# Decoder layer on one core: the operand buffers of TensorE moved to other addresses modulo 512 bytes

## The chip, the cores and the metric

The kernel runs on one core of a Trainium2 chip. The metric is the time on the device in microseconds (us); lower is better. Before the change the median of three runs was 2765.93 us (2765.84 to 2766.37).

## The reference

One decoder layer on x of 4 x 256 tokens and 512 features, with a context of 4 x 1601 tokens:

```
s = silu(x @ Wg.T); per token the 688 smallest |s| of 1376 are set to zero
x1 = layernorm(x + (s * (x @ Wu.T)) @ Wd.T)
q = rmsnorm(x1 @ Wq.T) per head (32 heads of 128);  k = rmsnorm(ctx @ Wk.T) (8 heads);  v = ctx @ Wv.T
x2 = layernorm(x1 + softmax(q @ k.T / sqrt(128) + mask) @ v @ Wo.T)   (1601 keys, 4 query heads a key head)
out = layernorm(x2 + the one chosen of 8 low-rank experts, rank 16)
```

## The kernel before, in words

All five engines run programs written out by hand, one after the other for six stages: gate and up projection, keys and values of the context (51 tiles of 128 tokens), down projection and norm, queries, attention (32 items of a batch and a key head, each in two units of two heads, 64 units in all), output projection with the experts. Semaphores set the order between engines; buffers have fixed places in the on-chip memory (SBUF).

Nearly every product is computed in three matmuls on operands split into a high and a low part of type float32r: hi by hi (line 158), hi by lo (159), lo by hi (160), in the helper `product` (lines 155 to 160). A matmul has a stationary operand of 128 x 128, which a weight load (PEld) brings into the array, and a moving operand of up to 512 columns, which streams through it. Each matmul has a weight load of its own. In a profile's row `banks<-kvw_hi,c_hi` the first name after the arrow is the moving operand and the second the stationary one.

Where the buffers stand: `chip.at(name, shape, place)` puts a tensor at byte 16512 + 4 x place of every partition, so place counts 4-byte words, and 128 words are 512 bytes. The constants AT_R0, AT_R1, AT_C, AT_X, AT_S and AT_P (16768, 28032, 39296, 43904, 46976, 49728) are multiples of 128 words, and so are the bare numbers in attention and output. Rows of 512, 1408 and 128 words keep it so. Before the change the moving and the stationary operand of every split matmul therefore start at the same place modulo 512 bytes: distance 0.

The buffers that the change touches, by stage:

- keys and values (`keys_and_values`): moving w_hi and w_lo (names kvw_hi, kvw_lo; one pair for K at AT_R0, one for V at AT_R1); stationary c_hi and c_lo, three slots used in turn, tile t in slot t mod 3; c_raw, which the DMA fills. Each tile makes 24 matmuls of 512 columns for K (2 blocks x 4 chunks x 3) and 24 for V.
- down projection: only p_sb (pd_sb), which makes room for V's buffer.
- attention (`attention`): moving k_hi and k_lo, two slots by item; stationary q_hi and q_lo. A score is 12 matmuls of 402 columns (4 blocks x 3), four scores a unit. The weighing of values (moving pT, stationary v) and the transposes (moving ident, stationary p_even or p_odd) are not touched.
- output (`output_and_experts`): moving wo_hi and wo_lo, eight pairs of buffers (QUAD_AT), one for each group of four heads; stationary o_hi and o_lo. 64 steps of 12 matmuls of 512 columns, eight steps with each pair.

The one product in which operands stood apart before is that of the experts at line 1926: expert_in's rows of 136 words start 0, 32, 64 and 96 bytes apart modulo 512 from x2T_sb.

Of the kernel before, what the change touches and what calls it, by code (L numbers as in the profile page):

```python
# [19 lines left out]
F32R = mybir.dt.float32r  # L20
U32 = mybir.dt.uint32

P = 128
B, S, D = 4, 256, 512
# [4 lines left out]
T = B * S  # L29
TT = T // P  # L30
CT = D // P
# [18 lines left out]
AT_ABS = 5760  # L50
AT_R0 = 16768
AT_R1 = 28032
AT_C = 39296
# [279 lines left out]
def keys_and_values(chip, abs_s, k_sb, WkT, WvT, ctxT, kS, vS, down):  # L333
# [7 lines left out]
    NB = N // 512  # L341
    RING = 3
# [4 lines left out]
    raw = chip.raw.rearrange("p (r n) -> p r n", r=IC)  # L347
    w_raw, first_c = raw[:, 0:SLOTS], raw[:, SLOTS].rearrange("p (c n) -> p c n", c=CT)
    sources = (WkT, WvT)
    w_hi = [chip.at(f"kvw_hi{m}", [P, NB, CT, 512], place, F32R) for m, place in enumerate((AT_R0, AT_R1))]  # L350
    w_lo = [chip.at(f"kvw_lo{m}", [P, NB, CT, 512], place + NB * CT * 512, F32R)
            for m, place in enumerate((AT_R0, AT_R1))]
    TAIL = 2 * NB * CT * 512
    flags = chip.at("flags", [P, 2, I], AT_R0 + TAIL, BF16)
    order = chip.at("order", [P, I], AT_R0 + TAIL + I)
    c_raw = chip.at("c_raw", [P, RING, CT, P], AT_C)

    HI_AT, LO_AT = (5, 6, 3), (7, 8, 4)
    c_hi = [chip.at(f"c_hi{s}", [P, CT, P], AT_C + 512 * HI_AT[s], F32R) for s in range(RING)]
    c_lo = [chip.at(f"c_lo{s}", [P, CT, P], AT_C + 512 * LO_AT[s], F32R) for s in range(RING)]  # L360
    square = chip.at("square", [P, N], AT_X)
    v_sb = chip.at("v_sb", [P, 2, N], AT_S)
    kT_sb = chip.at("kT_sb", [P, 2, N], AT_P)
# [329 lines left out]
def down_and_norm(chip, keep, x1T_hi, x1T_lo, x, WdT, pS, x1S, k_sb, queries):  # L693
# [3 lines left out]
    w_hi = chip.at("wd_hi", [P, IC, D], AT_R0, F32R)  # L697
    w_lo = chip.at("wd_lo", [P, IC, D], AT_R0 + IC * D, F32R)
    GN = IC * P
    hT_hi = [chip.at(f"hT_hi{s}", [P, GN], AT_C + GN * s, F32R) for s in range(2)]  # L700
    hT_lo = [chip.at(f"hT_lo{s}", [P, GN], AT_C + GN * (2 + s), F32R) for s in range(2)]
    p_sb = chip.at("pd_sb", [P, 2, GN], AT_R1 + 2 * CT * T)
    x_sb = chip.at("xd_sb", [P, 2, D], AT_X + 2 * 1024)
    y_sb = chip.at("yd_sb", [P, 2, D], AT_SMALL - 2 * D)
    x1_sb = chip.at("x1_sb", [P, 2, D], AT_X + 1024)
# [290 lines left out]


def queries(chip, x1T_hi, x1T_lo, WqT, qn, kn, qS, attention):


# [219 lines left out]
def attention(chip, mask, qS, kS, vS, oS, output):  # L1220
# [10 lines left out]
    SB, SW = 4, 402  # L1231
# [6 lines left out]
    RING = 4  # L1238
# [13 lines left out]
    p_sb = [chip.at("p_even", [P, QT, PP], 9088), chip.at("p_odd", [P, QT, PP], AT_R1)]  # L1252

    def pair(name, shape, *places):
        return [chip.at(f"{name}{s}", [P, *shape], place, F32R) for s, place in enumerate(places)]

    k_hi = pair("k_hi", (SB, 512), AT_C, AT_R0)
    k_lo = pair("k_lo", (SB, 512), AT_C + SB * 512, AT_R0 + SB * 512)
    q_hi = pair("q_hi", (2 * QW,), AT_C + 2 * SB * 512, AT_R0 + 2 * SB * 512)
    q_lo = pair("q_lo", (2 * QW,), AT_C + 2 * SB * 512 + 2 * QW, 48768)  # L1260
    v_hi = pair("v_hi", (NT * HD,), 45440, 49792)
# [403 lines left out]
def output_and_experts(chip, oS, x1S, WoT, AT, routeT, BwT, out):  # L1665
# [8 lines left out]
    W = 4 * P  # L1674
    RING = 3
    LEAD = RING - 1
    w_raw = raw[:, 0:WR * 2 * D].rearrange("p (r h n) -> p r h n", r=WR, h=2)
    o_raw = raw[:, WR * 2 * D:WR * 2 * D + OR * W].rearrange("p (r n) -> p r n", r=OR)
    QUAD_AT = (AT_C, AT_C + 8 * D, AT_ABS, AT_ABS + 8 * D, AT_ABS + 16 * D, 25088, 25088 + 8 * D, 25088 + 16 * D)
    w_hi = [chip.at(f"wo_hi{c}", [P, 4, D], QUAD_AT[c], F32R) for c in range(QUADS)]  # L1680
    w_lo = [chip.at(f"wo_lo{c}", [P, 4, D], QUAD_AT[c] + 4 * D, F32R) for c in range(QUADS)]
    o_hi = chip.at("o_hi", [P, RING, W], 22016, F32R)
    o_lo = chip.at("o_lo", [P, RING, W], 22016 + RING * W, F32R)
    y1_sb = chip.at("y1_sb", [P, 2, D], 18048)
    y2_sb = chip.at("y2_sb", [P, 2, D], 18048 + 2 * D)
    x2_sb = chip.at("x2_sb", [P, 2, D], 18048 + 4 * D)
# [258 lines left out]
def decoder_layer(nc, x, xT, ctxT, mask, WgT, WuT, WdT, WqT, WkT, WvT, WoT, qn, kn, routeT, AT, BwT, out):  # L1945
# [7 lines left out]
    with ExitStack() as whole:  # L1953
# [4 lines left out]
        x1T_lo = chip.at("x1T_lo", [P, CT, T], AT_R1 + CT * T, F32R)  # L1958

        output = output_and_experts(chip, oS, x1S, WoT, AT, routeT, BwT, out)  # L1960
        attend = attention(chip, mask, qS.rearrange("b g d h q -> (b g) d (h q)"), kS, vS, oS, output)
        query = queries(chip, x1T_hi, x1T_lo, WqT, qn, kn, qS, attend)
        down = down_and_norm(chip, abs_s, x1T_hi, x1T_lo, x, WdT, pS, x1S, k_sb, query)
        keys = keys_and_values(chip, abs_s, k_sb, WkT, WvT, ctxT, kS, vS, down)
        gate = gate_and_up(chip, abs_s, xT, WgT, WuT, pS, keys)

# [95 lines left out]
```

## Time and profile before

| | |
|---|---|
| median of three runs | 2765.93 us |
| time of the profiled execution | 2767.25 us |
| its span, first to last instruction | 2765.5 us |
| TensorE (PE) busy | 2722.0 us, 98% |
| weight loads (PEld) busy | 2364.3 us, 85% |
| VectorE, ScalarE, GpSimd busy | 74%, 49%, 37% |
| share of PE in the chain that ended last | 96% |
| granted TensorE clock, mean | 0.995 |

A matmul's record in the profile lasts from its start until its result is out, so the records of consecutive matmuls overlap; what a matmul costs is the time from its start to the start of the next. The timeline gives starts to 0.01 us, so a mean over several is read from the first and the last start of a stretch.

### The profile page before, as it was taken

The numbers are of one execution on the slowest core, as the hardware profiler recorded it, in microseconds if no ns is written. First come the engines' busy times: TensorE is split into PE (matmuls) and PEld (weight loads), VectorE is DVE, ScalarE is ACT, GpSimd is POOL, SyncE is SP. The second block draws the span as 40 slices with busy tenths as digits, with TensorE's granted clock in tenths as the row PEclk, the third lists the DMA queues.
The fourth block names the chain that finished last, engine by engine and source line by source line (L and its number), as shares of the span: only waits on it lengthen the run. The fifth ranks groups of instructions, "written<-read, shape, count | busy, mean of one in ns | idle before, by whom it ended". The sixth has DMA issues, their size and how long they took to land.

```text
span 2765.5 us, 45347 instructions
## 1 busy us (share of the span) xinstructions
PE 2722.0 (98%) x14624; PEld 2364.3 (85%) x14624; DVE 2055.5 (74%) x3054; ACT 1361.5 (49%) x2992; POOL 1009.9 (37%) x752
## 2 busy tenths in 40 slices
PE   8999999999999999999999999999999999999998
PEld 7888888888788878998998998999999999898786
DVE  2299999988855557777777777777777777777543
ACT  3243343334424445565666566666656666655421
POOL 1122222223313345444545444454444454541000
PEclk9999999999999999999999999999999999999999
DMA  5253333333333443111111111111111111111632
GB/s 177 83 181 108 112 111 107 114 114 114 95 124 114 125 128 98 55 53 54 51 60 55 62 55 62 55 62 55 62 55 58 52 49 58 55 43 61 210 107 73
DMA packets 252783, 239.49 MB, mean 87 GB/s; under 512 B 12084, under 2 KB 210772, under 8 KB 252728
## 3 DMA queue, kind: packets, MB, share of 16 engines
q1 hardware_dynamic: 252728, 238.81, 27.9%
q8 instruction: 28, 0.46, 0.1%
q14 instruction: 27, 0.22, 0.0%
HBM read 142.92 MB, written 95.85 MB: 86 GB/s over the span
## 4 chain that ended last, share of the span: by engine, by line
PE 96%; issue 2%; DVE 1%; POOL 1%; ACT 0%; DMA 0%; POOLq 0%; SPq 0%; DVEq 0%; ACTq 0%
PE banks L158 27%; PE banks L160 26%; PE banks L159 26%; PE banks L1616 13%; PE banks L322 2%; PE banks L1194 1%; PE banks L929 0%; PE banks L1926 0%; PE banks L1936 0%; POOL rstd_q L1094 0%; DVE p_even L1534 0%; DMA raw<-WoT_in 0%; POOL p_even L1427 0%; POOL x_lo L230 0%; DVE wo_lo L1825 0%
## 5 line engine op out<-in xcount | busy, mean ns | idle before, releaser
L1573 DVE TENSOR_TENSOR pT_lo<-banks,pT_hi 128x512 fp32r<-128x512 f32 (+1 forms) x832 | 573.6, 690 | 110.6 <-ACT pT_hi L1503 94.9
L1503 ACT CAST pT_hi<-banks 128x512 fp32r<-128x512 f32 (+1 forms) x576 | 333.7, 580 | 529.4 <-PE banks L1616 529.2
L559 DVE TENSOR_SCALAR_CACHE_REDUCE flags<-abs_s,cand 128x1376 bf16<-128x1376 f32 x248 | 393.2, 1642 | 1.1
L158 PE MATMUL banks<-k_hi,q_hi 128*128 128x402 f32 x1024 | 379.9, 371 | 0.0
L158 PE MATMUL banks<-pT_hi,v_hi 128*128 128x512 f32 (+1 forms) x832 | 374.0, 450 | 2.9 <-DVE pT_lo L1573 1.7
L159 PE MATMUL banks<-k_lo,q_hi 128*128 128x402 f32 x1024 | 357.2, 349 | 0.0
L160 PE MATMUL banks<-k_hi,q_lo 128*128 128x402 f32 x1024 | 355.8, 347 | 0.0
L160 PE MATMUL banks<-pT_hi,v_lo 128*128 128x512 f32 (+1 forms) x832 | 327.5, 394 | 0.0
L159 PE MATMUL banks<-pT_lo,v_hi 128*128 128x512 f32 (+1 forms) x832 | 326.6, 393 | 0.0
L1427 POOL TENSOR_SCALAR p_even<-p_even,p_inv 128x1601 f32<-128x1601 f32 x128 | 207.1, 1618 | 320.0 <-DVE p_inv L1541 320.0
L158 PE MATMUL banks<-kvw_hi,c_hi 128*128 128x512 f32 x816 | 322.6, 395 | 0.0
L160 PE MATMUL banks<-kvw_hi,c_lo 128*128 128x512 f32 x816 | 318.7, 391 | 0.0
L159 PE MATMUL banks<-kvw_lo,c_hi 128*128 128x512 f32 x816 | 317.9, 390 | 0.0
L1534 DVE CUSTOM_DVE_ANT_0 p_odd<-banks,minus_mask 128x1608 f32<-128x1608 f32 x128 | 234.6, 1833 | 105.4 <-PE banks L160 105.4
L1534 DVE CUSTOM_DVE_ANT_0 p_even<-banks,minus_mask 128x1608 f32<-128x1608 f32 x128 | 234.6, 1833 | 104.4 <-PE banks L160 104.4
L1427 POOL TENSOR_SCALAR p_odd<-p_odd,p_inv 128x1601 f32<-128x1601 f32 x128 | 206.9, 1617 | 211.4 <-DVE p_inv L1541 211.3
L1616 PEld LDWEIGHTS banks<-ident,p_even 128*128 128x128 f32 (+1 forms) x1664 | 207.9, 140 | 56.6 <-DVE qT_sb L1160 2.0
L1616 PEld LDWEIGHTS banks<-ident,p_odd 128*128 128x128 f32 (+1 forms) x1664 | 206.9, 140 | 55.9 <-POOL p_odd L1427 1.0
L1616 PE MATMUL banks<-ident,p_even 128*128 128x128 f32 (+1 forms) x1664 | 250.3, 273 | 1.8 <-DVE qT_sb L1160 1.8
L1616 PE MATMUL banks<-ident,p_odd 128*128 128x128 f32 (+1 forms) x1664 | 249.3, 272 | 0.6 <-POOL p_odd L1427 0.6
L1481 ACT ACTIVATE p_odd<-p_odd,t_min 128x1601 f32<-128x1601 f32 x128 | 209.9, 1640 | 41.3 <-DVE t_min L1534 41.3
L1481 ACT ACTIVATE p_even<-p_even,t_min 128x1601 f32<-128x1601 f32 x128 | 209.6, 1638 | 30.6 <-DVE t_min L1534 30.6
(160 smaller groups left out, 5316.2 us busy)
## 6 DMA issues: line engine op xcount, KB each, us to landing
raw<-keys SPq DMA_DIRECT2D x32, 800.5 KB, 4.5
values<-v_sb SPq DMA_DIRECT2D x50, 512.0 KB, 2.6
keys<-kT_sb SPq DMA_DIRECT2D x50, 512.0 KB, 4.4
raw<-values SPq DMA_DIRECT2D x32, 768.0 KB
queries<-qT_sb SPq DMA_DIRECT2D x64, 256.0 KB, 2.6
raw<-queries SPq DMA_DIRECT2D x32, 512.0 KB, 5.2
attended<-o_sb SPq DMA_DIRECT2D x128, 128.0 KB, 1.9
raw<-attended SPq DMA_DIRECT2D x64, 256.0 KB, 2.8
```

What stands on the lines that cost most here:

```text
L158: pe.matmul(out, a_hi, b_hi, start=start, stop=False)
L159: pe.matmul(out, a_hi, b_lo, start=False, stop=False)
L160: return pe.matmul(out, a_lo, b_hi, start=False, stop=stop)
L322: last = pe.transpose(banks[:, g * P:(g + 1) * P], k_sb[:, g * HD:(g + 1) * HD], chip.ident)
L559: bits.done(dve.tensor_scalar(flags[:, tt % 2], abs_s[:, tt], at[:, tt:tt + 1].bitcast(F32), 0.0, ALU.is_lt, ALU.add, accum_out=out[:, tt: ...
L1194: last = pe.transpose(psum[:, bank(i, s), h * P:(h + 1) * P], q_sb[:, s % 4, h * HD:(h + 1) * HD], ident)
L1427: pool.tensor_scalar(at, at, p_inv[:, n:n + 1], 1.0, ALU.mult, ALU.mult).then_inc(p_done, 1)
L1481: act.activation(at, at, ACT.Exp, bias=t_min[:, n:n + 1], scale=-1.0, accum_out=p_sum[:, n:n + 1]).then_inc(e_done, 1)
L1503: act.copy(pT_hi[0:rows(kt), m % RING], t_bank(m)[0:rows(kt)]).then_inc(pT_hi_act, 1)
L1534: dve.tensor_tensor_reduce(banked(p_sb[u % 2][:, j, 0:KP]), psum[:, 0:SB, 0:SW], banked(minus_mask[:, j % 2]), 1.0, 3.4028235e38, ALU.add, ...
L1573: dve.tensor_tensor(pT_lo[0:rows(kt), m % RING], t_bank(m)[0:rows(kt)], pT_hi[0:rows(kt), m % RING].bitcast(F32), ALU.subtract).then_inc(p ...
L1616: last = pe.transpose(t_bank(m)[0:rows(kt), P * j:P * (j + 1)], p_sb[u % 2][:, j, P * kt:P * kt + rows(kt)], ident)
```

## The change

Nothing is added, removed or put in another order: each engine's instruction rows are the same in both kernels, but for line numbers. Only places change. In words (of 4 bytes, modulo 128): V's moving weights go 64 up; the stationary slots of the context 8 down, 0 and 24 down, and c_raw 32 down; pd_sb one whole period of 128 up; k_hi and k_lo of the odd slot 40 down; the eight pairs of wo_hi and wo_lo 88, 24, 64, 48, 8, 80, 56 and 40 down; o_hi and o_lo one whole period down.

```
@@ -347,17 +347,18 @@
     raw = chip.raw.rearrange("p (r n) -> p r n", r=IC)
     w_raw, first_c = raw[:, 0:SLOTS], raw[:, SLOTS].rearrange("p (c n) -> p c n", c=CT)
     sources = (WkT, WvT)
-    w_hi = [chip.at(f"kvw_hi{m}", [P, NB, CT, 512], place, F32R) for m, place in enumerate((AT_R0, AT_R1))]
+    W_AT = (AT_R0, AT_R1 + 64)
+    w_hi = [chip.at(f"kvw_hi{m}", [P, NB, CT, 512], place, F32R) for m, place in enumerate(W_AT)]
     w_lo = [chip.at(f"kvw_lo{m}", [P, NB, CT, 512], place + NB * CT * 512, F32R)
-            for m, place in enumerate((AT_R0, AT_R1))]
+            for m, place in enumerate(W_AT)]
     TAIL = 2 * NB * CT * 512
     flags = chip.at("flags", [P, 2, I], AT_R0 + TAIL, BF16)
     order = chip.at("order", [P, I], AT_R0 + TAIL + I)
-    c_raw = chip.at("c_raw", [P, RING, CT, P], AT_C)
-
-    HI_AT, LO_AT = (5, 6, 3), (7, 8, 4)
-    c_hi = [chip.at(f"c_hi{s}", [P, CT, P], AT_C + 512 * HI_AT[s], F32R) for s in range(RING)]
-    c_lo = [chip.at(f"c_lo{s}", [P, CT, P], AT_C + 512 * LO_AT[s], F32R) for s in range(RING)]
+    c_raw = chip.at("c_raw", [P, RING, CT, P], AT_C - 32)
+
+    SLOT_AT = (AT_C + 5 * 512 - 8, AT_C + 7 * 512, AT_C + 3 * 512 - 24)
+    c_hi = [chip.at(f"c_hi{s}", [P, CT, P], SLOT_AT[s], F32R) for s in range(RING)]
+    c_lo = [chip.at(f"c_lo{s}", [P, CT, P], SLOT_AT[s] + 512, F32R) for s in range(RING)]
     square = chip.at("square", [P, N], AT_X)
     v_sb = chip.at("v_sb", [P, 2, N], AT_S)
     kT_sb = chip.at("kT_sb", [P, 2, N], AT_P)
@@ -699,7 +700,7 @@
     GN = IC * P
     hT_hi = [chip.at(f"hT_hi{s}", [P, GN], AT_C + GN * s, F32R) for s in range(2)]
     hT_lo = [chip.at(f"hT_lo{s}", [P, GN], AT_C + GN * (2 + s), F32R) for s in range(2)]
-    p_sb = chip.at("pd_sb", [P, 2, GN], AT_R1 + 2 * CT * T)
+    p_sb = chip.at("pd_sb", [P, 2, GN], AT_R1 + 2 * CT * T + P)
     x_sb = chip.at("xd_sb", [P, 2, D], AT_X + 2 * 1024)
     y_sb = chip.at("yd_sb", [P, 2, D], AT_SMALL - 2 * D)
     x1_sb = chip.at("x1_sb", [P, 2, D], AT_X + 1024)
@@ -1254,8 +1255,8 @@
     def pair(name, shape, *places):
         return [chip.at(f"{name}{s}", [P, *shape], place, F32R) for s, place in enumerate(places)]
 
-    k_hi = pair("k_hi", (SB, 512), AT_C, AT_R0)
-    k_lo = pair("k_lo", (SB, 512), AT_C + SB * 512, AT_R0 + SB * 512)
+    k_hi = pair("k_hi", (SB, 512), AT_C, AT_R0 - 40)
+    k_lo = pair("k_lo", (SB, 512), AT_C + SB * 512, AT_R0 - 40 + SB * 512)
     q_hi = pair("q_hi", (2 * QW,), AT_C + 2 * SB * 512, AT_R0 + 2 * SB * 512)
     q_lo = pair("q_lo", (2 * QW,), AT_C + 2 * SB * 512 + 2 * QW, 48768)
     v_hi = pair("v_hi", (NT * HD,), 45440, 49792)
@@ -1676,11 +1677,12 @@
     LEAD = RING - 1
     w_raw = raw[:, 0:WR * 2 * D].rearrange("p (r h n) -> p r h n", r=WR, h=2)
     o_raw = raw[:, WR * 2 * D:WR * 2 * D + OR * W].rearrange("p (r n) -> p r n", r=OR)
-    QUAD_AT = (AT_C, AT_C + 8 * D, AT_ABS, AT_ABS + 8 * D, AT_ABS + 16 * D, 25088, 25088 + 8 * D, 25088 + 16 * D)
+    QUAD_AT = (AT_C - 88, AT_C + 8 * D - 24, AT_ABS - 64, AT_ABS + 8 * D - 48, AT_ABS + 16 * D - 8,
+               24832 + 256 - 80, 25088 + 8 * D - 56, 25088 + 16 * D - 40)
     w_hi = [chip.at(f"wo_hi{c}", [P, 4, D], QUAD_AT[c], F32R) for c in range(QUADS)]
     w_lo = [chip.at(f"wo_lo{c}", [P, 4, D], QUAD_AT[c] + 4 * D, F32R) for c in range(QUADS)]
-    o_hi = chip.at("o_hi", [P, RING, W], 22016, F32R)
-    o_lo = chip.at("o_lo", [P, RING, W], 22016 + RING * W, F32R)
+    o_hi = chip.at("o_hi", [P, RING, W], 21888, F32R)
+    o_lo = chip.at("o_lo", [P, RING, W], 21888 + RING * W, F32R)
     y1_sb = chip.at("y1_sb", [P, 2, D], 18048)
     y2_sb = chip.at("y2_sb", [P, 2, D], 18048 + 2 * D)
     x2_sb = chip.at("x2_sb", [P, 2, D], 18048 + 4 * D)
```

## Rows read from the trace of the kernel before

**Rows 1.** Page: busy time, share and instructions; granted clock; shares of the chain.

```profile
PE 2722.0 (98%) x14624; PEld 2364.3 (85%) x14624; DVE 2055.5 (74%) x3054; ACT 1361.5 (49%) x2992; POOL 1009.9 (37%) x752
...
PEclk9999999999999999999999999999999999999999
...
PE 96%; issue 2%; DVE 1%; POOL 1%; ACT 0%; DMA 0%; POOLq 0%; SPq 0%; DVEq 0%; ACTq 0%
```

**Rows 2.** Groups by line and shape: matmuls touched, with busy and mean ns.

```profile
L158 PE MATMUL banks<-k_hi,q_hi 128*128 128x402 f32 x1024 | 379.9, 371 | 0.0
...
L158 PE MATMUL banks<-kvw_hi,c_hi 128*128 128x512 f32 x816 | 322.6, 395 | 0.0
...
L158 PE MATMUL banks<-wo_hi,o_hi 128*128 128x512 f32 x256 | 105.1, 410 | 2.1 <-DVE wo_lo L1825 2.1
```

**Rows 3.** Timeline of PE in keys and values: start us, us, what.

```profile
399.85 0.39 PE L158 MATMUL banks<-kvw_hi,c_hi 128*128 128x512 f32 x1
400.07 0.39 PE L159 MATMUL banks<-kvw_lo,c_hi 128*128 128x512 f32 x1
...
403.93 0.39 PE L158 MATMUL banks<-kvw_hi,c_hi 128*128 128x512 f32 x1
```

**Rows 4.** The same groups' weight loads, and those of the transposes.

```profile
L159 PEld LDWEIGHTS banks<-k_lo,q_hi 128*128 128x128 f32 x1024 | 196.0, 191 | 0.0
...
L1616 PEld LDWEIGHTS banks<-ident,p_odd 128*128 128x128 f32 x1536 | 191.1, 140 | 51.5 <-POOL p_odd L1427 1.0
...
L159 PEld LDWEIGHTS banks<-kvw_lo,c_hi 128*128 128x128 f32 x816 | 153.5, 188 | 30.3
```

**Rows 5.** Timeline of PE over one score of attention.

```profile
1502.24 0.35 PE L159 MATMUL banks<-k_lo,q_hi 128*128 128x402 f32 x1
...
1502.99 0.34 PE L160 MATMUL banks<-k_hi,q_lo 128*128 128x402 f32 x1
1503.16 0.34 PE L158 MATMUL banks<-k_hi,q_hi 128*128 128x402 f32 x1
1503.34 0.35 PE L159 MATMUL banks<-k_lo,q_hi 128*128 128x402 f32 x1
...
1504.28 0.39 PE L158 MATMUL banks<-pT_hi,v_hi 128*128 128x512 f32 x1
```

**Rows 6.** Timeline of PE in gate and up.

```profile
104.45 0.40 PE L158 MATMUL banks<-w_hi,x_hi 128*128 128x512 f32 x1
...
105.16 0.39 PE L158 MATMUL banks<-w_hi,x_hi 128*128 128x512 f32 x1
105.38 0.39 PE L159 MATMUL banks<-w_lo,x_hi 128*128 128x512 f32 x1
...
105.85 0.32 PE L158 MATMUL banks<-w_hi,x_hi 128*128 128x352 f32 x1
```

**Rows 7.** Timeline of PE around transposes of keys.

```profile
645.85 1.04 PE L322 MATMUL banks<-ident,k_sb 128*128 128x128 f32 x8
646.65 0.47 PE L158 MATMUL banks<-kvw_hi,c_hi 128*128 128x512 f32 x1
```

**Rows 8.** Timeline of PE in the output stage, around the experts' product.

```profile
2657.77 0.39 PE L159 MATMUL banks<-wo_lo,o_hi 128*128 128x512 f32 x1
...
2660.30 1.09 PE L1926 MATMUL banks<-expert_in,x2T_sb 128*128 128x136 f32 x8
2661.14 0.48 PE L158 MATMUL banks<-wo_hi,o_hi 128*128 128x512 f32 x1
```

**Rows 9.** Three stretches: busy us by engine: keys, attention, output.

```profile
core 0: us, PE busy (x) PEld busy (x) DVE busy (x) ACT busy (x) POOL busy (x), PEclk, DMA share, GB/s
160.00:700.00 540.00, 540.00 (x2567) 450.85 (x2566) 501.45 (x687) 211.90 (x874) 149.77 (x138) 1.00 0.38 113
1044.00:2526.00 1482.00, 1481.54 (x8701) 1337.31 (x8702) 1167.92 (x1817) 896.31 (x1282) 709.96 (x405) 1.00 0.19 58
2600.00:2720.00 120.00, 120.00 (x555) 97.46 (x554) 57.33 (x128) 28.09 (x51) 6.98 (x12) 1.00 0.35 106
```

More of the change, by code:

```diff
@@ L349, in keys_and_values @@
     sources = (WkT, WvT)
-    w_hi = [chip.at(f"kvw_hi{m}", [P, NB, CT, 512], place, F32R) for m, place in enumerate((AT_R0, AT_R1))]
+    W_AT = (AT_R0, AT_R1 + 64)
+    w_hi = [chip.at(f"kvw_hi{m}", [P, NB, CT, 512], place, F32R) for m, place in enumerate(W_AT)]
     w_lo = [chip.at(f"kvw_lo{m}", [P, NB, CT, 512], place + NB * CT * 512, F32R)
-            for m, place in enumerate((AT_R0, AT_R1))]
+            for m, place in enumerate(W_AT)]
     TAIL = 2 * NB * CT * 512
@@ L355, in keys_and_values @@
     order = chip.at("order", [P, I], AT_R0 + TAIL + I)
[L356 to L360, printed above, removed]
+    c_raw = chip.at("c_raw", [P, RING, CT, P], AT_C - 32)
+    SLOT_AT = (AT_C + 5 * 512 - 8, AT_C + 7 * 512, AT_C + 3 * 512 - 24)
+    c_hi = [chip.at(f"c_hi{s}", [P, CT, P], SLOT_AT[s], F32R) for s in range(RING)]
+    c_lo = [chip.at(f"c_lo{s}", [P, CT, P], SLOT_AT[s] + 512, F32R) for s in range(RING)]
     square = chip.at("square", [P, N], AT_X)
@@ L701, in down_and_norm @@
     hT_lo = [chip.at(f"hT_lo{s}", [P, GN], AT_C + GN * (2 + s), F32R) for s in range(2)]
-    p_sb = chip.at("pd_sb", [P, 2, GN], AT_R1 + 2 * CT * T)
+    p_sb = chip.at("pd_sb", [P, 2, GN], AT_R1 + 2 * CT * T + P)
     x_sb = chip.at("xd_sb", [P, 2, D], AT_X + 2 * 1024)
@@ L1255, in pair @@
         return [chip.at(f"{name}{s}", [P, *shape], place, F32R) for s, place in enumerate(places)]
-    k_hi = pair("k_hi", (SB, 512), AT_C, AT_R0)
-    k_lo = pair("k_lo", (SB, 512), AT_C + SB * 512, AT_R0 + SB * 512)
+    k_hi = pair("k_hi", (SB, 512), AT_C, AT_R0 - 40)
+    k_lo = pair("k_lo", (SB, 512), AT_C + SB * 512, AT_R0 - 40 + SB * 512)
     q_hi = pair("q_hi", (2 * QW,), AT_C + 2 * SB * 512, AT_R0 + 2 * SB * 512)
@@ L1678, in output_and_experts @@
     o_raw = raw[:, WR * 2 * D:WR * 2 * D + OR * W].rearrange("p (r n) -> p r n", r=OR)
-    QUAD_AT = (AT_C, AT_C + 8 * D, AT_ABS, AT_ABS + 8 * D, AT_ABS + 16 * D, 25088, 25088 + 8 * D, 25088 + 16 * D)
+    QUAD_AT = (AT_C - 88, AT_C + 8 * D - 24, AT_ABS - 64, AT_ABS + 8 * D - 48, AT_ABS + 16 * D - 8,
+               24832 + 256 - 80, 25088 + 8 * D - 56, 25088 + 16 * D - 40)
     w_hi = [chip.at(f"wo_hi{c}", [P, 4, D], QUAD_AT[c], F32R) for c in range(QUADS)]
     w_lo = [chip.at(f"wo_lo{c}", [P, 4, D], QUAD_AT[c] + 4 * D, F32R) for c in range(QUADS)]
-    o_hi = chip.at("o_hi", [P, RING, W], 22016, F32R)
-    o_lo = chip.at("o_lo", [P, RING, W], 22016 + RING * W, F32R)
+    o_hi = chip.at("o_hi", [P, RING, W], 21888, F32R)
+    o_lo = chip.at("o_lo", [P, RING, W], 21888 + RING * W, F32R)
     y1_sb = chip.at("y1_sb", [P, 2, D], 18048)
```

## The prediction

> **What bounds the kernel now.** I read the page first: TensorE is busy for 98% of the span and makes up 96% of the chain that ended last, at a granted clock of 9 tenths or more in every slice, which is the 2.4 GHz level [rows 1]. So the time is the number of matmuls times the time from one start to the next. Then the groups by line and shape, for the counts [rows 2]. Their mean of 371 to 410 ns is no cost, since the records overlap; the cost has to be read from the starts in the timeline. In the keys stage 18 matmuls of 512 columns follow each other from 399.85 to 403.93, 4.08 us, that is 226.7 ns each, with line 158, 159 and 160 alike [rows 3]. At 2.4 GHz 512 columns stream in 512 / 2.4 = 213.3 ns, so 13.3 ns of each are something else. In a score 11 matmuls of 402 columns go from 1502.24 to 1504.28, 2.04 us, 185.5 ns each [rows 5], against 402 / 2.4 = 167.5: 18.0 ns are something else. The excess does not grow with the columns, so it goes with the matmul, and each matmul has a weight load of 128 columns beside it.
>
> Next I asked whether the excess is contention between the two streams that read on-chip memory. Two rows speak for it. A weight load takes 188 to 191 ns beside a split matmul and 140 beside a transpose, 48 to 51 ns less [rows 4]. And matmuls of one shape, all at distance 0, do not all cost the same: in a score two in a row take 0.35 us (175 ns each, from 1502.99 to 1503.34), the last five 0.94 (188 each) [rows 5]; in the gate stage one takes 0.22 us (105.16 to 105.38) while six around it take 1.40 (233.3 each) [rows 6]; in the output stage, after an interruption, 11 take 2.53 (230.0 each, 2657.77 to 2660.30) [rows 8]. Something that depends on how the two streams fall against each other in time moves a 512-column matmul between about 220 and 233 ns and a 402-column one between 175 and 188. A distance in the address could act on the same thing. That it does is not shown by any row.
>
> **The change, part by part.** No instruction is added, removed or reordered on any engine, and sizes and counts stay, so only durations can change.
>
> Matmuls whose distance changes: K's projection in slots 0 and 2, 34 of 51 tiles x 24 = 816; slot 1 keeps distance 0 (17 x 24 = 408 do not change). V's projection, all 51 x 24 = 1224. Scores of the odd slot: 16 of 32 items x 2 units x 4 scores x 12 = 1536, half of the 3072, three lines of 1024 each [rows 2]. The output projection, 64 x 12 = 768, three lines of 256 each [rows 2]. That is 2808 matmuls of 512 columns and 1536 of 402, 4344 of 14624 [rows 1]. The moves of o_hi, o_lo and pd_sb are by a whole period and cost nothing at any distance; the gate, down and query stages, the weighing of values and the transposes keep distance 0.
>
> The price of one is not in the trace, since no split matmul stands at another distance there. I bound it from both sides.
> - Fastest: if the excess went entirely, 2808 x 13.3 = 37.3 us and 1536 x 18.0 = 27.6 us, 65 us in all. The best that the trace shows for such shapes is 0.22 us and 175 ns [rows 5, 6]; with 0.22 taken at its full 6.7 ns below 226.7 that is 2808 x 6.7 = 18.8 us and 1536 x 10.5 = 16.1 us, 35 us in all.
> - Slowest: the slow stretches, 233.3 and 188.0 ns [rows 5, 6]: 2808 x 6.6 = 18.5 us and 1536 x 2.5 = 3.8 us, 22 us in all. Nothing excludes that a bad distance costs more than any stretch at distance 0. As an outer end, the weight load's own 48 ns [rows 4] on every one of them would be 4344 x 48 = 209 us; I give it little weight, since the excess at distance 0 is a quarter of that.
>
> The value I take: eight different distances will not all be the best one, so a third of the 35 us of the best stretches, 12 us. The reason for the sign is that at distance 0 both streams begin at the same place modulo 512 at the same time: the weight load that follows starts with the matmul before it, in nearly every case, and its 512 bytes and the first 512 bytes of the moving row coincide. A distance takes that coincidence away. It is a weak reason, and I say so.
>
> Other engines don't take this gain away. In the keys stretch VectorE is busy 501.45 of 540 us, in attention 1167.92 of 1482, in the output stage 57.33 of 120, while TensorE fills all three [rows 9]. The closest cover is in the keys stage: VectorE could follow a TensorE that is up to 7% faster (38.55 / 540), and even the whole excess is 13.3 / 226.7 = 5.9%. So a gain on TensorE there is a gain of the kernel. A loss is one in any case.
>
> The sum against the profiled execution: 2767.25 - 12 = 2755; that execution is 1.3 us above the median of the runs (2765.93), so in terms of the median 2754.
>
> One rule speaks against the change. The row: of 226.7 ns per matmul, 13.3 are not streaming [rows 3]. The Trainium skill, TensorE: Matmul & The Clock Gate, section "Step-by-step: what each phase is for", says that the engine has two independent read ports and that loading the next weights takes no read bandwidth from the running matmul; by that no address can matter. By that rule the time stays at 2766. The same page, "LDWEIGHTS (loading the stationary operand)", sets 128 columns at 128 / 1.2 = 107 ns; the trace has 140 and 188 ns, longer beside a full-rate stream, which the rule does not account for, so it does not settle the matter.
>
> **The rivals.**
> - No change. The excess is a price of swapping weights, or of two streams that share something whatever their addresses. For it: the streams move at different rates (the moving one reads 2048 bytes in the time of a matmul, the weight load 512), so each passes the other modulo 512 whatever distance they start at, and a distance would only say when. Also the only product at other distances, that of the experts with 0, 32, 64 and 96 bytes, takes 0.84 us for eight of 136 columns, and the transposes of keys at distance 0 take 0.80 for eight of 128 [rows 7, 8]: 1.05 against 136 / 128 = 1.06, so no distance is felt there. But those run at half the rate (about 100 ns for 128 columns against 53 at 2.4 GHz), where there may be nothing to collide. Against it: the spread between 175 and 188 ns at one and the same distance. The time: 2766.
> - Slower. At distance 0 the matmul leaves the weight load behind from the first column; at a distance at which the load's place lies a little ahead, the moving stream runs into it and stays behind it. The place is the start of each of the 4344 matmuls. It decides once the mean over the new distances is more than 1.3 ns above now (5.5 us / 4344). For it: the long runs in keys sit at 226.7, below the 230 and 233 of unsettled stretches [rows 3, 6, 8], so distance 0 is already a good state there, and a spread of distances is more likely to be worse than a good state than better. Against it: scores do not sit at a good state, and they go down to 175. Price: half of the slow stretches to all of them, 11 to 22 us; I take 14: 2780. A bad distance beyond what rows show would give 2790 and more.
> - The full gain: every new distance takes the excess away. For it only the 175 ns in a score, which is 7.5 above streaming. 2766 - 65 to 2766 - 35 is 2701 to 2731.
>
> **How the numbers follow.** Two executions differ by some tenths of a us, and 0.2%, 5.5 us, is about what a measurement tells from no change. Faster by a part (2735 to 2760) 0.33, and by the full gain 0.08: faster 0.41. No change 0.26. Slower 0.33, of which 0.08 is beyond 2788. The likeliest single one is the part gain, 2754. The range leaves out the full gain and the far slow end, and little more: 2730 to 2788. The likeliest case's own range is 2735 to 2760.
>
> **What would show it.** Start to start in the timeline, by stage. If I am right, V's projection and the output stage lie below 226.7 ns, with differences between the eight groups of the output stage; scores of odd items lie below 185.5 on average and those of even items stay; K's slot 1 stays at 226.7 while slots 0 and 2 move. The weight loads' 188 to 191 ns fall where the starts come closer. If all stay, the first rival holds. If untouched matmuls (gate, transposes, values) move, my whole account of where the effect can act is wrong; if VectorE gets waits in the keys stage, its cover was thinner than the busy share says.

## The result: slower by 0.85%

The changed kernel takes 2789.97 us in the median of four runs (2789.73 to 2791.42), the kernel before 2766.15 beside it; the ratio is 1.0085, with a 95% interval of 1.0073 to 1.0097. The forecast was 2754 us, within 2730 to 2788. The time lies just above the range, and on the other side of no change: a gain was forecast and a loss came.

The page of the changed kernel first: busy time by engine, granted clock, shares of the chain.

```profile
PE 2744.1 (98%) x14624; PEld 2365.4 (85%) x14624; DVE 2055.2 (74%) x3054; ACT 1362.8 (49%) x2992; POOL 1011.6 (36%) x752
...
PEclk9999999999999999999999999999999999999999
...
PE 95%; issue 2%; DVE 1%; POOL 1%; ACT 0%; DMA 0%; SPq 0%; POOLq 0%; DVEq 0%; ACTq 0%
```

Against [rows 1] nothing moved but TensorE: its span is 2787.9 us (2765.5 before), its busy time 22.1 us longer with the same 14624 matmuls, the clock at the same level, VectorE and the others within 2 us. The same three stretches as in [rows 9], busy us by engine:

```profile
core 0: us, PE busy (x) PEld busy (x) DVE busy (x) ACT busy (x) POOL busy (x), PEclk, DMA share, GB/s
160.00:700.00 540.00, 540.00 (x2524) 443.03 (x2523) 492.88 (x682) 208.23 (x855) 147.12 (x136) 1.00 0.37 111
1044.00:2526.00 1482.00, 1474.98 (x8600) 1325.09 (x8601) 1156.15 (x1799) 889.83 (x1274) 714.97 (x410) 1.00 0.19 58
2600.00:2720.00 120.00, 120.00 (x542) 96.20 (x542) 59.32 (x121) 32.61 (x54) 5.92 (x10) 1.00 0.39 126
```

TensorE still fills the stretches of keys and output and begins 2524 matmuls instead of 2567 in the first and 542 instead of 555 in the last. (The second stretch now begins before attention runs at full pace, since everything is later.) So the time went into the matmuls themselves, and the timeline of TensorE shows into which. K's projection of one tile in slot 0 and of the next in slot 1, first and last row of each, then V's in slot 1, its third, twelfth and last row:

```profile
492.41 0.40 PE L158 MATMUL banks<-kvw_hi,c_hi 128*128 128x512 f32 x1
...
497.77 0.39 PE L160 MATMUL banks<-kvw_hi,c_lo 128*128 128x512 f32 x1
...
504.48 0.39 PE L158 MATMUL banks<-kvw_hi,c_hi 128*128 128x512 f32 x1
...
509.69 0.40 PE L160 MATMUL banks<-kvw_hi,c_lo 128*128 128x512 f32 x1
...
511.26 0.40 PE L160 MATMUL banks<-kvw_hi,c_lo 128*128 128x512 f32 x1
...
513.34 0.39 PE L160 MATMUL banks<-kvw_hi,c_lo 128*128 128x512 f32 x1
...
516.06 0.40 PE L160 MATMUL banks<-kvw_hi,c_lo 128*128 128x512 f32 x1
```

K in slot 0, 8 words off, takes 5.36 us (497.77 - 492.41) for 23 matmuls, 233 ns each; K in slot 1, which kept distance 0, takes 5.21, 226.5 ns, as in [rows 3]. V in slot 1 stands 64 words (256 bytes) off and takes 4.80 us for 21, 228.6 ns: 231.1 in the first nine of them, soon after an interruption by transposes, and 226.7 in the last twelve (2.72 us). At a distance of 8 words no such flat stretch comes: by the unrounded starts of this trace K in slot 0 repeats 235, 233, 234, 231 ns to the end of its run. So the distance decides into which pattern a run falls.

Two scores of the odd slot, one right after the other, ten starts each:

```profile
1749.47 0.34 PE L159 MATMUL banks<-k_lo,q_hi 128*128 128x402 f32 x1
...
1751.32 0.35 PE L160 MATMUL banks<-k_hi,q_lo 128*128 128x402 f32 x1
...
1754.04 0.35 PE L159 MATMUL banks<-k_lo,q_hi 128*128 128x402 f32 x1
...
1756.05 0.37 PE L160 MATMUL banks<-k_hi,q_lo 128*128 128x402 f32 x1
```

That is 1.85 and 2.01 us, 184 (1.842 us by the unrounded starts) and 201 ns per matmul, at one and the same distance; in [rows 5] it was 185. And in the output stage two of the eight groups, 40 words off (first pair) and 16 modulo 64 (second pair):

```profile
2648.08 0.39 PE L159 MATMUL banks<-wo_lo,o_hi 128*128 128x512 f32 x1
...
2650.41 0.40 PE L160 MATMUL banks<-wo_hi,o_lo 128*128 128x512 f32 x1
...
2657.80 0.39 PE L159 MATMUL banks<-wo_lo,o_hi 128*128 128x512 f32 x1
...
2660.09 0.40 PE L160 MATMUL banks<-wo_hi,o_lo 128*128 128x512 f32 x1
```

233 and 229 ns. Every start of the trace taken together (means from the start of a matmul to the next start, in ns, from unrounded starts; interrupted ones left out):

| group | distance in words (moving - stationary) | before | after | matmuls |
|---|---|---|---|---|
| K slot 0, 2 | 8, 24 | 226.8, 226.7 | 233.4, 233.4 | 816 |
| K slot 1 | 0 | 226.7 | 226.7 | 408 |
| V slot 0, 2 | 72, 88 | 227.8, 227.9 | 233.4, 233.1 | 816 |
| V slot 1 | 64 | 227.8 | 228.5 | 408 |
| scores, odd items | 88 | 185.0 | 190.1 | 1536 |
| scores, even items | 0 | 184.9 | 184.9 | 1536 |
| output, groups 0 to 7 | 40, 104, 64, 80, 120, 48, 72, 88 | 227.0 to 229.7 | 233.2, 234.3, 230.4, 228.9, 233.1, 233.4, 232.9, 234.3 | 96 each |

816 x 6.7 = 5.5 us for K, 816 x 5.4 + 408 x 0.7 = 4.7 for V, 1536 x 5.1 = 7.8 for scores, and 768 at a mean of 4.5 in the output make 3.5: 21.5 of the 22.4 us by which the span grew. Not all of that is as neat as it looks. With the interrupted starts counted too, keys and values take 10.0 us more, scores 6.4 (594.6 to 601.0), the output stage 1.8, and the weighing of values, which the change does not touch, 2.8 (625.2 to 628.0; 228.7 to 231.4 ns each). But attention at its old places comes in two states: in the kernels below that leave it alone, scores take 592.4 and 591.8 us and the weighing of values 627.6 and 627.9 (keys only, output only), the same sum as 594.6 and 625.2 to 0.2 us. Against those kernels attention lost 9 us, nearly all of it in scores.

The weight loads, whose times I had taken for a sign of contention [rows 4], still take 191, 140 and 188 ns:

```profile
L159 PEld LDWEIGHTS banks<-k_lo,q_hi 128*128 128x128 f32 x1024 | 196.0, 191 | 1.0
...
L1617 PEld LDWEIGHTS banks<-ident,p_odd 128*128 128x128 f32 x1536 | 191.2, 140 | 51.9 <-POOL p_odd L1428 1.0
...
L159 PEld LDWEIGHTS banks<-kvw_lo,c_hi 128*128 128x128 f32 x816 | 153.3, 188 | 33.6
```

### The profile page after: what moved, and what is told of

The parts are those of the page before. It is cut to its first block, busy times and chain, and to the rows that moved or that the text cites. A ratio compares the mean times of both kernels' runs of the same rounds, so it can differ in the third digit from the quotient of the medians.

```text
span 2787.9 us, 45347 instructions
## 1 busy us (share of the span) xinstructions
PE 2744.1 (98%) x14624; PEld 2365.4 (85%) x14624; DVE 2055.2 (74%) x3054; ACT 1362.8 (49%) x2992; POOL 1011.6 (36%) x752
## 4 chain that ended last, share of the span: by engine, by line
PE 95%; issue 2%; DVE 1%; POOL 1%; ACT 0%; DMA 0%; SPq 0%; POOLq 0%; DVEq 0%; ACTq 0%
PE banks L158 27%; PE banks L160 26%; PE banks L159 26%; PE banks L1617 13%; PE banks L322 2%; PE banks L1195 1%; PE banks L930 0%; DMA raw<-WoT_in 0%; PE banks L1928 0%; PE banks L1938 0%; POOL rstd_q L1095 0%; DVE p_even L1535 0%; POOL p_even L1428 0%; DVE wo_lo L1827 0%; DVE p_odd L1535 0%
```

## The experiments

Each ran beside the kernel before on the same chip. The parts and the pair are measured in several runs each; the kernels with half loads, other load lengths or narrower rows leave out a part of the products, so they were run once, and only their starts are read. First the question whether it is the distance at all.

**Both operands moved alike.** K's and V's weights and the context slots, k and q of the odd slot, and all operands of the output stage stand 88 words (40 down, which is the same modulo 128) off their old places, so the distance is 0 again. Three buffers of other engines and q_lo of the odd slot move to make room. Lines of the edit against the kernel before, others left out (...):

```
-    ... for m, place in enumerate((AT_R0, AT_R1))]
+    ... for m, place in enumerate((AT_R0 + 88, AT_R1 + 88))]
...
+    SLOT_AT = (AT_C + 5 * 512 - 40, AT_C + 7 * 512 - 40, AT_C + 3 * 512 - 40)
...
-    k_hi = pair("k_hi", (SB, 512), AT_C, AT_R0)
+    k_hi = pair("k_hi", (SB, 512), AT_C + (0), AT_R0 + (88))
...
+    q_hi = pair("q_hi", (2 * QW,), AT_C + 2 * SB * 512, AT_R0 + 2 * SB * 512 + 88)
+    q_lo = pair("q_lo", (2 * QW,), AT_C + 2 * SB * 512 + 2 * QW, 24064 + 88)
...
+    QUAD_AT = (AT_C - 40, AT_C + 8 * D - 40, AT_ABS - 40, ...
+    o_hi = chip.at("o_hi", [P, RING, W], 21976, F32R)
```

> Here the places of both operands move by the same 88 (or 40 down) words in keys and values, in the odd items of attention and in the output stage, so no start stands on a multiple of 256 bytes, and the distance is 0 everywhere. Theory D (only the distance between moving and stationary operand counts): start to start stays 226.7 ns in the settled runs of keys and values and in the output stage, 185 ns in scores of both slots, and the kernel takes 2766 us, as before. Theory P (an operand that starts off a multiple of 256 bytes is read more slowly, by itself): 233 ns and 190 ns as in the changed kernel, also where that kernel kept 226.7 (K of slot 1, 408 matmuls), and at least 2790 us.

Measured: 2767.42 us, ratio 0.9998 (0.9988 to 1.0007). K of slot 0 in the timeline, first and last of its 24 matmuls:

```profile
487.20 0.39 PE L158 MATMUL banks<-kvw_hi,c_hi 128*128 128x512 f32 x1
...
492.41 0.39 PE L160 MATMUL banks<-kvw_hi,c_lo 128*128 128x512 f32 x1
```

5.21 us for 23 matmuls, 226.5 ns; over all tiles K has 226.7 in every slot, and scores of the odd slot 184.2. V has 228.4 to 228.5 for 227.8 before, a difference that lies in the ten matmuls after each interruption. So at this place, 88 words on, the place by itself costs next to nothing; the distance does. Theory P falls.

**Other distances.** The same edits with other numbers; four of the output groups use a distance that is no multiple of 8 words, by a slice of a buffer that is allocated a little lower. The places in short (a list, not the code):

```
w_hi, w_lo: AT_R0, AT_R1 + 32;  SLOT_AT: -16, 0, -32;  k_hi, k_lo: AT_C - 16, AT_R0 - 32
QUAD_AT: -112, -96, -124, -116, -68, -108, -32, -16
```

> Other distances (moving minus stationary, words): K 16, 0, 32 and V 48, 32, 64 in slots 0, 1, 2; scores -16 in even items, -32 in odd ones; output groups 16, 32, 4, 12, 60, 20, 96, 112. Theory D with a period of 256 bytes (64 words), as the changed kernel's groups suggest: V slot 2 (64) stays at 226.7, like K slot 1 (0); V slot 0 (48) is at 233; K slot 0, output groups 0 and 7 at 16 and 112 (48) give 229 and 233; the not yet measured 32 and 96 are alike, and by that theory K slot 2, V slot 1 and output groups 1 and 6 agree within 1 ns. With a period of 512 bytes 32 and 96 differ, and so do 0 and 64. Rival T (the distance acts only on timing, each group's mean is one of many states): the groups of one distance differ among stages. Whole kernel: between 2770 and 2790 us by D; no value below 226.7 is expected by the thought that 0 is the best state, one or more below it if 0 is only one state among many.

Measured: 2780.58 us, ratio 1.0042 (1.0026 to 1.0059). K in slot 0 (16 words), K in slot 2 (32), V in slot 2 (64):

```profile
491.89 0.39 PE L158 MATMUL banks<-kvw_hi,c_hi 128*128 128x512 f32 x1
...
497.16 0.39 PE L160 MATMUL banks<-kvw_hi,c_lo 128*128 128x512 f32 x1
...
515.77 0.39 PE L158 MATMUL banks<-kvw_hi,c_hi 128*128 128x512 f32 x1
...
521.14 0.39 PE L160 MATMUL banks<-kvw_hi,c_lo 128*128 128x512 f32 x1
...
522.71 0.39 PE L160 MATMUL banks<-kvw_hi,c_lo 128*128 128x512 f32 x1
...
527.51 0.39 PE L160 MATMUL banks<-kvw_hi,c_lo 128*128 128x512 f32 x1
```

5.27 us for 23 (229 ns), 5.37 (233 ns) and 4.80 for 21 (229 ns). With the groups of the changed kernel, the means by distance modulo 64 words (one word is 4 bytes) are as follows, with 0 standing for the places of the kernel before and 64 for moved groups:

| distance, words | 0 | 64 | 4 | 8 | 12 | 16 | 20 | 24 | 32 | 40 | 48 | 56 | 60 |
|---|---|---|---|---|---|---|---|---|---|---|---|---|---|
| ns at 512 columns | 226.7 (K), 227.8 (V), 227.0 to 229.7 (output) | 228.5, 228.9 (V), 230.4 (output) | 231.7 | 232.9 to 233.4 | 232.5 | 228.9 to 229.1 | 231.1 | 233.1 to 234.3 | 231.9 to 233.1 | 233.2, 234.3 | 232.6 to 233.4 | 233.1 | 235.9 |

Where groups of different stages share a distance other than 0 modulo 64 they agree within 1.2 ns, and groups at 64 words lie only 0.7 to 1.1 ns above their own value at 0 (V slot 1 and output group 2 of the changed kernel, V slot 2 here, where theory D had expected 226.7; V moved alike at distance 0 also had 228.5), so the period is 256 bytes, not 512, and rival T falls for matmuls of 512 columns. The state is not wholly the group's own: K's slot 1, still at 0, has 227.6 in this kernel. By the unrounded starts its runs begin with 226, 235, 228, 234, 231 ns and stay near 226.7 from about the eighth matmul on; in the changed kernel, where they follow an unsettled run of V as well, they have 226.7 from the start. Of K's and V's runs in this trace too only those at 0 and 64 words reach that value; the others end in patterns of their own, K at 16 words in one of 225 to 233 ns, K at 32 in one of 228 to 239. Of the distances tried none is better than 0 at 512 columns; 16 words (64 bytes) come next. Scores take 186.0 ns at 32 words (odd items) and 183.4 at 48 (even items).

**The parts alone.** Each with the diff of the change for that stage and the other stages as before.

> The change in keys and values alone. Theory D: K slots 0 and 2 and V slots 0 and 2 at 233.2 to 233.4 ns, slot 1 at 226.7 and 228.5, the rest as before: 4 x 408 matmuls x 6.2 ns = 10 us, so 2776 us. If the stages influenced each other (VectorE later in keys, for one), it would be another sum.

Measured: 2776.66 us, ratio 1.0030 (1.0018 to 1.0042); profiled span 2775.0, 9.5 more than before. All six slots as in the changed kernel within 0.1 ns.

> The change of k_hi and k_lo of the odd slot alone. Theory D: scores of odd items at 190.1 ns for 185.0, 1536 x 5.1 = 7.8 us, and the matmul after a score up to 2 us in all: 2774 to 2776 us. Rival: the loss in attention is taken up by slack there (TensorE idles 0.5 of 1482 us there before, so hardly any): 2766 to 2768.

Measured: 2777.18 us, ratio 1.0035 (1.0023 to 1.0046); span 2775.4, 9.9 more. Odd scores 189.8 ns, even ones 184.9: TensorE has no slack that takes this loss up.

> The change of the output stage alone: the eight groups as in the changed kernel (233 ns but for those at 64 and 80 words, at 230.4 and 228.9), 96 matmuls each, 3 to 4 us in all: 2769 to 2770 us. With keys alone (+9.5) and attention alone (+10) the sum makes the whole change's 22 to 24 us if the parts do not influence each other.

Measured: 2770.91 us, ratio 1.0012 (1.0002 to 1.0021); span 2770.0, 4.5 more. The groups are within 0.5 ns of the changed kernel's. The three spans add up to 23.9 us, the whole change to 22.4. Single executions of one kernel differ by more than these 1.5 us (2763.8 to 2769.3 for the span of the kernel before, run beside the keys and attention kernels), so no influence of the parts on each other is seen.

**Is it what the weight load reads?** Half of the stationary columns from the second tile on, first at the old places, then at the changed ones. This leaves out half of the rows of each product (a memset of the banks at the start makes the rows that are not written defined):

```
-    last = product(pe, out[:, j * 512:(j + 1) * 512], c_hi[s % RING][:, c], c_lo[s % RING][:, c],
+    m = P if first else P // 2
+    last = product(pe, out[0:m, j * 512:(j + 1) * 512], c_hi[s % RING][:, c, 0:m], c_lo[s % RING][:, c, 0:m],
```

> From tile 1 on, keys and values load only 64 of the 128 stationary columns and so compute only half of each product's rows (the other rows keep older values); places are those of the kernel before, distance 0. Moving columns stay 512. Theory L (the excess over 213.3 ns is what the weight load's reads take from the moving stream): about half as many reads, so the settled start to start falls from 226.7 to about 220 ns. Rival W (a fixed price of swapping weights): it stays at 226.7.

Measured: 2771.80 us in one run. The weight loads of 64 columns, then K in slot 0 at distance 0:

```profile
L159 PEld LDWEIGHTS banks<-kvw_lo,c_hi 128*64 128x64 f32 x800 | 107.5, 134 | 71.3
```

```profile
490.79 0.40 PE L158 MATMUL banks<-kvw_hi,c_hi 128*64 128x512 f32 x1
...
496.08 0.40 PE L160 MATMUL banks<-kvw_hi,c_lo 128*64 128x512 f32 x1
```

The load takes 134 ns for 188, but the matmuls take 5.29 us for 23, 230 ns: more than with the whole load, not less. Theory L fails, and so does the rival W, which expected 226.7.

> The same halved weight loads, at the changed kernel's places. Theory L: the loss by distance halves as well: slots 0 and 2 at about 223 to 224 ns, 3 above slot 1 (6.7 with full loads). Rival W: slots 0 and 2 keep the full 6.7 ns above slot 1. A second rival: a distance only matters where the two streams start together, then the difference is independent of the load's length too.

Measured: 2786.53 us in one run. K in slot 0 (8 words) and in slot 1 (0):

```profile
491.74 0.39 PE L158 MATMUL banks<-kvw_hi,c_hi 128*64 128x512 f32 x1
...
497.05 0.39 PE L160 MATMUL banks<-kvw_hi,c_lo 128*64 128x512 f32 x1
...
503.69 0.39 PE L158 MATMUL banks<-kvw_hi,c_hi 128*64 128x512 f32 x1
...
508.98 0.39 PE L160 MATMUL banks<-kvw_hi,c_lo 128*64 128x512 f32 x1
```

5.31 and 5.29 us; over the tiles with half loads 230.8, 230.0 and 231.4 ns for slots 0, 1 and 2. The loss by distance nearly goes, but because distance 0 loses its advantage. Neither rival had said so.

**Widths.** The places of the changed kernel, with narrower moving rows in keys and values from the second tile on, so that the rest of the output's columns is left out; in the next run (384, 416) stands for (448, 402):

```
+    n = 512 if first else (448, 402)[which]
+    ... out[:, j * 512:j * 512 + n], ..., w_hi[which][:, j, c, 0:n], w_lo[which][:, j, c, 0:n]
```

> Places of the changed kernel; from tile 1 on K's matmuls stream 448 of 512 columns and V's 402 (the rest of the output keeps older values), with whole weight loads. Slots 0 and 2 stand 8 and 24 words off modulo 64, slot 1 stands at 0. Theory M (a matmul settles at streaming + 13.3 ns if its distance and its width are multiples of 64 words, and otherwise wanders about 16 to 20 ns over streaming): K slot 1 at 448 / 2.4 + 13.3 = 200.0 ns, K slots 0 and 2 at 203 to 207; V slot 1 at 402 / 2.4 + 16 to 18 = 184 to 185.5, as the scores of the kernel before, V slots 0 and 2 at 187 to 190. Rival N (width is of no account, the scores' higher excess comes from something else in attention): V slot 1 at 167.5 + 13.3 = 180.8.

Measured: 2747.48 us in one run. V with 402 columns in slot 1, 21 matmuls apart:

```profile
487.30 0.34 PE L160 MATMUL banks<-kvw_hi,c_lo 128*128 128x402 f32 x1
...
491.16 0.34 PE L160 MATMUL banks<-kvw_hi,c_lo 128*128 128x402 f32 x1
```

3.86 us, 183.8 ns. Over the narrowed tiles 183.7 in slot 1, 184.5 and 188.5 in slots 0 and 2; K with 448 columns has 204.7, 203.0 and 205.3 in slots 0, 1 and 2. So at 402 columns 8 words cost V only 0.8 ns, less than theory M had. By the unrounded starts a run of V in slot 1 goes 189, 184, 176, 179, 183, 186, 191, 187, 185, 175, 180, ... ns, the sequence of the scores of the kernel before (186, 190, 188, 185, 176, 178, 183, 186, 191, 188). So the scores' higher excess over streaming comes from their width, and rival N falls; but 448 at distance 0 is 203.0, not the settled 200.0 that theory M had.

> The same with K's matmuls 384 wide and V's 416. Theory M: K slot 1 at 160 + 13.3 = 173.3 ns and settled, V slot 1 (416 is no multiple of 64) at 173.3 + 16 to 18 = 189 to 191. Rival N: V slot 1 at 186.6.

Measured: 2751.47 us in one run. K with 384 columns in slot 0, 8 words off:

```profile
468.72 0.34 PE L158 MATMUL banks<-kvw_hi,c_hi 128*128 128x384 f32 x1
...
472.71 0.34 PE L160 MATMUL banks<-kvw_hi,c_lo 128*128 128x384 f32 x1
```

3.99 us for 23, 173.5 ns; over the narrowed tiles 173.3, which is 13.3 above the 160.0 of streaming (384 / 2.4) and settled, at a distance that is bad for 512 columns. (The settled values at 384 and 512 columns, 173.3 and 226.7, differ by 53.4 ns for 128 columns, which is 2.4 columns a ns; that is the sense in which 13.3 ns are not streaming.) Slot 1 (distance 0) has a mean of 174.6 and settles at 173.3 late in a run, slot 2 has 176.5; V with 416 has 187.4, 188.3 and 193.0, so 8 words (slot 0) are a little better than 64 (slot 1). Theory M's rule on the multiple of 64 words fails here.

**Load lengths.** The edit of the halved load with (32, 96)[which] for P // 2, at the places of the changed kernel; K computes only 32 rows of each product and V 96.

> Places of the changed kernel; moving rows of 512, but K loads 32 stationary columns and V 96 (the other rows of the output keep older values). With 64 columns all slots were at 230 to 231 and the loss by distance had shrunk from 6.7 to 1 ns. Theory L2 (the loss by distance is what two streams do to each other while both run, and needs a load of the whole period): K with 32 columns shows no difference between slots (under 1 ns); V with 96 lies between, 2 to 5 ns. Rival (only loads of all 128 columns are special): V with 96 shows under 1 ns too. In both, a fixed price of 12 to 17 ns per matmul stays even with a quarter of the load, if it is not the load's reading that makes it.

Measured: 2790.27 us in one run. V with 96 stationary columns, in slot 0 (72 words) and slot 1 (64), 18 matmuls apart:

```profile
500.50 0.39 PE L160 MATMUL banks<-kvw_hi,c_lo 128*96 128x512 f32 x1
...
504.58 0.39 PE L160 MATMUL banks<-kvw_hi,c_lo 128*96 128x512 f32 x1
...
512.40 0.39 PE L160 MATMUL banks<-kvw_hi,c_lo 128*96 128x512 f32 x1
...
516.54 0.39 PE L160 MATMUL banks<-kvw_hi,c_lo 128*96 128x512 f32 x1
```

4.08 and 4.14 us, 226.7 and 230.0 ns: the state that whole loads have at distance 0 now appears at 72 words, and 64 is the worse one. Slot 2 has 232.9. K with 32 columns: 232.6, 231.6 and 233.4. Both theories had under 1 ns between K's slots; for V, theory L2 had 2 to 5 ns with slot 1 the best, and the rival under 1. Both fail. The load of 32 columns takes 108 ns on the average, 64 columns 134, 96 columns 161 and 128 columns 188, which is 26 to 27 ns for every 32 columns and about 81 ns besides.

**Transposes and scores at further distances.** k_hi and k_lo at AT_C - 48 and AT_R0 - 16, p_even at 9088 + 40; the kernel before otherwise.

> Scores at distances 16 (even items) and 48 (odd items, -16) in words modulo 64; p_even 40 words up, so the transposes of even units stand 24 words off. Theory D with the price only where the moving stream runs at full rate: transposes of p_even stay at 109 ns, as those of p_odd. Rival: they rise by 5 ns, 1536 x 5 = 8 us. Scores: at -16 the sweep had 183.4 ns against 183.9 to 185.0 at distance 0, so if that is a real gain and not the run's own, odd items are near 183.4 again and even ones between 183 and 190; the kernel takes 2765 to 2774 us.

Measured: 2768.03 us, ratio 1.0005 (0.9995 to 1.0015). The matmuls of the transposes, 24 words off (p_even) and at 0 (p_odd), busy us and mean ns:

```profile
L1616 PE MATMUL banks<-ident,p_even 128*128 128x128 f32 x1536 | 230.9, 273 | 1.8 <-DVE qT_sb L1160 1.8
L1616 PE MATMUL banks<-ident,p_odd 128*128 128x128 f32 x1536 | 230.0, 272 | 0.6 <-POOL p_odd L1427 0.6
```

273 and 272 ns as before, and 109 ns from start to start within a group of four in both. These matmuls run at about half rate (109 ns for 128 columns), and there this distance is not felt. Scores: 184.3 ns at 16 words, 183.6 at 48 (183.4 in the sweep), while distance 0 had 185.0, 184.2, 184.1 and 184.0 in four kernels whose attention was the same (the kernel before, half loads at distance 0, keys only, output only). A gain of 0.4 ns against a spread of 1.0 is none that I can show.

**Another width for the scores.** `SB, SW = 4, 402` of the kernel before becomes 404 or 408.

> The kernel before, with scores in four blocks of 404 columns for 402 (three more padding keys each in all, same results), distance 0. Streaming is 168.3 ns. Theory M (what a matmul pays above streaming depends on width, distance and load length together, between a settled 13.3 ns and about 20): 181.7 ns if it settles, 184.1 as now if it wanders at 16 on the average; 3072 matmuls make -7 to +0 us, so 2759 to 2767 us. Rival (more columns only cost more): 185.0, +2.6 us, 2769 us.

Measured: 2765.34 us, ratio 0.9997 (0.9988 to 1.0006). A score of the odd slot:

```profile
1728.67 0.34 PE L159 MATMUL banks<-k_lo,q_hi 128*128 128x404 f32 x1
...
1730.49 0.34 PE L160 MATMUL banks<-k_hi,q_lo 128*128 128x404 f32 x1
```

1.82 us for ten, 182 ns; over all scores 183.1 with two columns more, 14.8 above streaming for 16.5 to 17.5. With all starts counted the scores take 6.4 us less than in the kernel before, but the weighing of values takes 3.1 us more and the transposes 1.2, and the median is 1.2 us lower: no version that beats the kernel before beyond its interval.

> The same with blocks of 408 columns, 170.0 ns of streaming. Theory M: 183.3 ns if settled (-2.5 us), up to 188 if not (+12 us): 2764 to 2778 us. Rival (a fixed 16.6 over streaming): 186.6, +7.7 us, 2774 us.

Measured: 2771.45 us, ratio 1.0017 (1.0008 to 1.0026); scores 184.7 ns, below the 186.6 of the rival, yet the kernel is 5 us slower. The trace has it outside the scores: all starts counted, they take 0.3 us less than in the kernel before, the weighing of values 3.2 more and the transposes 1.3 more, 4.2 of the 4.6 us by which the span grew. The kernel with 404 columns has the same surplus there and is not slower because its scores save 6.4 us.

> Blocks of 404 columns with k_hi and k_lo 16 words down in even items and 32 words down in odd ones. Theory M: another pair of means than at distance 0, each between 181.7 and 190 ns, and not the same for both. If the means at distance 0 and here agree within 0.5 ns, distance has no say at this width.

Measured: 2770.29 us, ratio 1.0013 (1.0004 to 1.0022); 183.1 ns at 48 words modulo 64 in even items, 186.3 at 32 in odd ones. So distance has a say at this width too, and 0 and 48 are equal; the 3.2 ns on the 1536 odd scores are 4.9 us, the difference to the kernel with 404 columns at distance 0.

## Why the prediction was wrong

- Where the effect can act was right in the main: the 4344 matmuls whose distance changed. Gate, queries, transposes and K's slot 1 stayed within 1 us each. The weighing of values did move (2.8 us), which the prediction had called a sign against its whole account; but it has the same time in kernels that leave attention alone, so it is a second state of that stage and not an effect of the change. That no other engine covers a loss was right as well (the parts alone add up).
- The slow end of the bounds was 6.6 ns for 512 columns, where 6.7 was measured in K and a mean of 4.9 over all 2808, and 2.5 for scores, where 5.1 was measured. That the slow ends add up to 22 us and the span grew by 22.4 is luck: the term for scores was too small (3.8 us for 7.8) and the one for 512 columns too large (18.5 for 13.7).
- Two readings of [rows 6] behind these bounds were not sound. The six starts that take 1.40 us include the one of 0.22; the other five take 1.18, 236 ns each and not 233.3, which would have put the slow end at 9.3 ns and 26 us for 512 columns, and 2790 inside the range. And the best stretch, 0.22 us, is a single difference of two times rounded to 0.01, so it can't be told from 226.7; 18.8 of the 35 us from which the gain was taken rest on it.
- The step that failed is the sign: "A distance takes that coincidence away", and with it the 12 us of gain in the sum. It took starts at the same place for the bad case, and they are the good one: 226.7 ns at distance 0 in K, 233.4 at 8 and 24 words, 226.7 again when both operands move alike. The rival had read the rows better: the long runs at 226.7 are a settled state [rows 3], and the 230 and 233 ns of unsettled stretches [rows 6, 8] are what other distances give. That row was in hand, and it weighed less than a picture of two streams that no row showed.
- The rival's mechanism, a moving stream that stays stuck behind the weight load, is not shown either. A shorter load should then have cost less, and it did not; and the weight load's 188 ns did not move with the distance. The prediction read 188 against 140 ns [rows 4] as contention. Beside full-rate matmuls the part of the load's time that does not go with its columns is the same 81 ns from 32 to 128 columns, so it does not grow with what the load reads, and it is no sign of reads in each other's way.
- The rule that speaks against any effect (the Trainium skill, TensorE: Matmul & The Clock Gate, section "Step-by-step: what each phase is for": loading the next weights takes no read bandwidth from the running matmul) would have given 2766. The measurement differs: at full rate a change of place alone costs up to 7 ns a matmul (output group 7: 227.1 to 234.3). At half rate, at the one distance tried (24 words), the trace agrees with it. Which part of that rule fails is not shown, since the weight load's own time did not change.
- The tails were too thin: 2790 us is 2 above the range, and 0.08 had been given to all beyond it.
- One number ahead of the prediction is off: 49728 (AT_P) stands 64 words off a multiple of 128. No operand of a matmul stands there, so the count of 4344 and the distances hold.

What stays open: why. The runs show that the price over streaming (13.3 to 22.6 ns at 512 columns and whole loads) depends jointly on distance, width and length of the load, and on what ran before (scores of one kernel at 184 and 201 ns). They don't show what the two streams share.

## What to carry to other kernels

Where float32r matmuls with a weight load each fill TensorE, and the shape is 512 moving and 128 stationary columns, keep moving and stationary operands at the same place modulo 256 bytes; every other distance tried cost 0.7 to 3.2% of the matmul here. For other shapes the good distance is another: with 96 stationary columns 72 words gave 227.3 ns and 64 gave 230.0, and 384 moving columns settled at 8 words. Read the steady start to start of each shape from long runs of the timeline; if it sits flat at one value lower than that of interrupted stretches, the layout is in a good state, and a change of address is more likely to lose it than to improve it. Compare a part with the same part of more than one kernel, since attention alone had two states with scores 1 ns apart. And measure at one distance in one stage before moving the buffers of three.

## What the runs showed of the hardware

- The price by distance has a period of 256 bytes: V takes 227.8 to 228.5 ns at 0 words and 228.5 at 64, and K at 8 words and V at 72 take 233.4 alike.
- After an interruption V's runs at 0 or 64 words take about ten matmuls (229.5 to 231 ns on the average) until they are flat at 226.7; at 8 words (K) and 72 (V) runs stay in a pattern of 231 to 235.
- It is the distance and not the place: K with both operands 352 bytes off together takes 226.7 ns.
- Half of the weight load does not make the matmul cheaper: 230.0 ns for 226.7 at distance 0.
- The cost of a matmul in a long run repeats in a pattern; at 402 columns the pattern of 176 to 191 ns was the same in attention and, with other buffers, in V's projection.
- One distance can have several states: scores 88 words off took 184, 192, 195 or 201 ns each, in an order that recurs over the scores.
